# Recurrence output of a fused audio-tower layer: one clamped exponential, no GpSimd products, divisor and sigmoid inverted together

## The chip, the cores and the metric

The kernel runs on one core of a Trainium2 chip, as one program from inputs in memory to output in memory. The metric is the device time of one execution in microseconds (us). The engines are TensorE (PE: matmuls and transposes), VectorE (DVE), ScalarE (ACT: activation functions), GpSimd (POOL) and SyncE (SP, which issues most DMAs here). Each engine runs its own list of instructions in order and meets the others only through semaphores.

## The reference

The input x is 32 sequences of 750 steps with 256 channels, float32.

```
h = wavelet low pass with stride 2, twice, along time          # 32 x 750 x 256 -> 32 x 192 x 256
n = layernorm(h);  k = n @ Wk.T;  r = n @ Wr.T;  v = r
w = -exp(time_decay);  u = time_first                          # per channel
for each step t:                                               # (a, b, pp) start at 0, 0, -1e38
    q  = max(pp, u + k_t);  e1 = exp(pp - q);  e2 = exp(u + k_t - q)
    y_t = (e1 * a + e2 * v_t) / (e1 * b + e2)
    q2 = max(pp + w, k_t);  f1 = exp(pp + w - q2);  f2 = exp(k_t - q2)
    a, b, pp = f1 * a + f2 * v_t, f1 * b + f2, q2
h = h + (sigmoid(r) * y) @ Wo.T
n2 = layernorm(h);  the 2 best of 8 experts by n2 @ router_w + router_b, gates by softmax
h = h + sum over the two of gate * (relu(n2 @ W1 + b1) @ W2 + b2)
```

## The kernel before, in words

The program has two stages. `tokens_to_experts` does everything up to the routing, `experts` does the expert matmuls, the gather of tokens by lists and the accumulation into the output. The change touches only the first.

The first stage takes the 32 sequences two at a time, as 16 pairs. The five steps of a pair are spread over five rounds: `rounds` calls `body(p0, p1, p2, p3, p4)` for rounds 0 to 19 on every engine, with pair p0 in step 0 (wavelet filter and layernorm statistics), p1 in step 1 (transposes and the projections k and r), p2 in step 2 (the recurrence), p3 in step 3 (output projection, second layernorm) and p4 in step 4 (routing, token lists). A step whose pair doesn't exist in a round is left out: p2 exists in rounds 2 to 17 and p4 in rounds 4 to 19.

With channels on partitions, a pair is 128 x 4 rows (two halves of the channels, two sequences) of 192 steps, so most recurrence tiles have 768 elements in a partition, or 772 where one column is put in front. DVE works the recurrence as scans along time: `pp` (add and max) at L605, `sbb` and `sa` (multiply and add) at L643 and L646. Around them stand, in the kernel before:

- `dl` = k + u - pp (L613, two instructions, since u differs by half), `dn_s` (L621, two), and on ACT `up_s`, `e2s`, `e1s` (L367 to L371) for the state, and `e2y`, `e1y` (L380, L383: a relu and an exponential each) for the output.
- POOL forms the products `t2` = e2y * v (L332) and `t3` = e1y * sbb (L338); DVE forms `t1` = e1y * sa (L666), `num` = t1 + t2 (L681), `den` = t3 + e2y (L690) and `dsg` = den * (1 + exp(-r)) (L693, with `er` from L385 and L683).
- ACT forms `inv` = exp(-ln(dsg)) (L428, L431), and in the next round DVE forms `oT` = num * inv (L628, two instructions).

POOL also runs a chain of four tiny operations for each layernorm (`rstd`, L319 to L325), from the statistics that DVE's `bn_aggr` (L587) gives to the scale and bias that ACT uses, and at the end of its round it issues six indirect DMAs (L346) that write the token lists of p4. They wait for the 24th of the 25 routing steps. The routing steps are small DVE instructions on 3 to 24 elements (among them `is_second`, L759); `route_to(k)` issues those up to number k, which scatters them between the large ones of the round.

PE's order in a round is: the first part of the wavelet (`conv_first`, L468), the transposes for p1, `project(p3)` (L483, which waits for oT), the rest of the wavelet (`conv_rest`, L474), k and r for p1 with `ranks` between them, the transposes for p3, the last of r, and the router logits (L530). ACT copies the finished wavelet to `h` (L389); DVE takes `bn_stats` of it (L672) for p0.

Of the kernel before, what the change touches and what calls it, by code (L numbers as in the profile page):

```python
# [22 lines left out]
ALU = mybir.AluOpType  # L23
# [8 lines left out]
P = 128  # L32
# [34 lines left out]
EMAX = 2.0 ** 54  # L67

# [63 lines left out]
def tokens_to_experts(nc, x, taps, taps_down, wkT, wrT, woT, decay, first, rw, rb, out, rows, lists, tables):  # L132
# [12 lines left out]
    with ctx:  # L145
# [4 lines left out]
        w, uw, nuw = sb("w", [P, HC]), sb("uw", [P, HC]), sb("nuw", [P, HC])  # L150
# [11 lines left out]
        c_eps, c_pow, c_neg = sb("c_eps", [P, 3]), sb("c_pow", [P, 3]), sb("c_neg", [P, 3])  # L162
        zrow, nobody = sb("zrow", [P, R * C]), sb("nobody", [P, LIST // P], U32)
# [49 lines left out]
        setup_act, pads = sem("setup_act"), sem("pads")  # L213
        x_loaded = [sem("x_loaded0"), sem("x_loaded1")]
# [9 lines left out]
        diffs, clamped, exps, state, t2_done, t3_done = sem("diffs"), sem("clamped"), sem("exps"), sem("state"), sem("t2_done"), sem("t3_done")  # L224
# [5 lines left out]
        N_LN1, N_LN2, N_DIFF, N_STATE, N_ROUTE, N_RSTD = 6, 7, 5, 8, 25, 4  # L230
# [64 lines left out]
        def _(pool):  # L295
# [948 lines left out]
```

## Time and profile before

| | |
|---|---|
| median of 3 runs | 1180.82 us |
| lowest, highest | 1174.84, 1181.34 us |
| profiled execution: span from first to last instruction | 1179.9 us |
| first stage | up to about 412 us of the span |
| busy share of the span: PE, DVE, ACT, POOL | 85%, 79%, 56%, 62% |
| mean granted TensorE clock | 0.934 of full |

The profiled execution is one execution; its span is 0.9 us under the median of the runs. The shares are means over both stages, which have different limits, so the stage has to be read by itself: by busy time in a window, and by the order of instructions in time.

### The profile page before, as it was taken

To read this page: it belongs to the slowest core of one execution; us is meant where nothing else is said; L and a number is where in the kernel's file an instruction comes from. 1 tells how busy PE (TensorE), PEld (TensorE's weight loads), DVE (VectorE), ACT (ScalarE), POOL (GpSimd) and SP (SyncE) were. 2 spreads that over 40 slices of the span, in tenths; PEclk is the share of its full clock that TensorE was granted. 3 is DMA by queue.
4 is the path that set the end of the run, shared out by engine and by line. 5 is a ranking of instruction groups with operands and counts; after the bars stand their busy time and mean duration, and the time that the engine had idled before them with its cause. 6 is when DMAs were issued, how large, how long until landed. Compare 5 with 4: busy or idle time off the path is not lost.

```text
span 1179.9 us, 21997 instructions
## 1 busy us (share of the span) xinstructions
PE 1008.8 (85%) x6244; PEld 917.8 (78%) x6244; DVE 931.9 (79%) x2350; ACT 656.6 (56%) x1253; POOL 735.6 (62%) x634
## 2 busy tenths in 40 slices
PE   6878878887874329999999999999999999999994
PEld 5656646666643229999999999999999999999994
DVE  2899999999998437878778877878878788787872
ACT  2767757666755125556555555555555555555651
POOL 1458778778778434565665657566565655656563
PEclk9898998888976559999999999999999999999997
DMA  7334235235111145565655647565574655646572
GB/s 240 99 97 132 82 100 141 81 94 131 43 41 41 41 175 171 133 189 146 171 177 131 188 129 190 152 163 182 126 191 135 182 168 144 187 127 188 147 170 29
DMA packets 76131, 160.78 MB, mean 136 GB/s; under 512 B 12781, under 2 KB 65518, under 8 KB 70986
## 3 DMA queue, kind: packets, MB, share of 16 engines
q0 software_dynamic: 34592, 120.55, 37.3%
q1 hardware_dynamic: 41514, 39.95, 11.6%
q8 instruction: 10, 0.16, 0.1%
q14 instruction: 15, 0.12, 0.0%
HBM read 131.81 MB, written 28.65 MB: 136 GB/s over the span
## 4 chain that ended last, share of the span: by engine, by line
issue 15%; POOL 15%; DVE 12%; PE 10%; DMA 8%; DVEq 1%; ACT 1%; POOLq 1%; ACTq 0%
POOL out_rows L995 8%; DMA out_rows<-yout,dest 7%; PE acc L1083 5%; PE hp L1072 5%; DVE wlo L1120 3%; POOL b2s L958 3%; POOL tid L948 3%; DVE ysum L1197 3%; DVE hhi L1172 2%; DVE xlo L1124 1%; DVE hlo L1174 1%; DMA raw<-in_ew,idx 1%; POOL raw L945 1%; DVE gA L1140 1%; PE xt L1063 0%
## 5 line engine op out<-in xcount | busy, mean ns | idle before, releaser
L1041 ACT ACTIVATE hid<-hp,b 128x384 f32<-128x384 f32 x312 | 180.4, 578 | 318.7 <-PE hp L1072 318.1
L1083 PE MATMUL acc<-whi,hhi 128*128 128x256 f32 x936 | 266.2, 284 | 29.4 <-DVE hlo L1174 29.4
L1083 PE MATMUL acc<-wlo,hhi 128*128 128x256 f32 x936 | 261.5, 279 | 0.0
L1083 PE MATMUL acc<-whi,hlo 128*128 128x256 f32 x936 | 261.4, 279 | 0.0
L1072 PE MATMUL hp<-xhi,whi 128*128 128x384 f32 x624 | 215.4, 345 | 2.2 <-DVE xlo L1124 2.2
L995 POOL DMA_INDIRECT out_rows<-yout,dest x117 | 185.8, 1588 | 47.7 <-issue 35.1
L1120 DVE TENSOR_TENSOR wlo<-raw,whi 128x512 fp32r<-128x512 f32 x312 | 213.0, 684 | 0.8 <-ACT whi L1016 0.8
L1072 PE MATMUL hp<-xlo,whi 128*128 128x384 f32 x624 | 211.0, 338 | 0.0
L1072 PE MATMUL hp<-xhi,wlo 128*128 128x384 f32 x624 | 211.0, 338 | 0.0
L1016 ACT ACTIVATE whi<-raw 128x512 fp32r<-128x512 f32 x312 | 194.3, 624 | 28.7 <-DMA raw<-in_ew,idx 28.7
L1083 PEld LDWEIGHTS acc<-whi,hhi 128*128 128x128 f32 x936 | 175.4, 187 | 42.6 <-issue 27.7
L1172 DVE CAST hhi<-hid 128x384 fp32r<-128x384 f32 x312 | 117.1, 375 | 83.3 <-ACT hid L1041 75.4
L1174 DVE TENSOR_TENSOR hlo<-hid,hhi 128x384 fp32r<-128x384 f32 x312 | 174.1, 558 | 10.8
L1083 PEld LDWEIGHTS acc<-wlo,hhi 128*128 128x128 f32 x936 | 175.8, 188 | 0.0
L1083 PEld LDWEIGHTS acc<-whi,hlo 128*128 128x128 f32 x936 | 175.6, 188 | 0.0
L945 POOL DMA_INDIRECT raw<-in_ew,idx x40 | 46.9, 1172 | 176.0 <-issue 165.3
L954 POOL DMA_INDIRECT xg<-token_rows,tid x120 | 125.2, 1043 | 46.7 <-issue 44.0
L346 POOL DMA_INDIRECT expert_lists<-tid,slots x96 | 131.6, 1371 | 30.9 <-issue 26.2
L1072 PEld LDWEIGHTS hp<-xhi,whi 128*128 128x128 f32 x624 | 117.8, 189 | 3.7 <-DVE xlo L1124 2.6
L1072 PEld LDWEIGHTS hp<-xhi,wlo 128*128 128x128 f32 x624 | 118.0, 189 | 0.0
L1072 PEld LDWEIGHTS hp<-xlo,whi 128*128 128x128 f32 x624 | 117.6, 188 | 0.0
L468 PE MATMUL conv_ps<-xin,filt 128*128 128x256 f32 x256 | 67.4, 423 | 3.0 <-DVE wseq L576 1.6
(174 smaller groups left out, 1715.9 us busy)
## 6 DMA issues: line engine op xcount, KB each, us to landing
xin<-in_x SPq DMA_DIRECT2D x32, 512.0 KB
xin<-in_x SPq DMA_DIRECT2D x32, 256.0 KB
token_rows<-xs SPq DMA_DIRECT2D x16, 259.0 KB
out_rows<-h SPq DMA_DIRECT2D x16, 256.0 KB, 3.3
token_rows<-xs SPq DMA_DIRECT2D x32, 64.8 KB
out_rows<-h SPq DMA_DIRECT2D x32, 64.0 KB, 4.1
xg<-token_rows,tid POOLq DMA_INDIRECT x120
out_rows<-yout,dest POOLq DMA_INDIRECT x117
```

The costliest lines, as they stand in the source:

```text
L346: pool.indirect_dma_start(lists, bass.IndirectOffsetOnAxis(slots[:, p4.s, c:c + 1], 0), tid[:, p4.s, c % 3:c % 3 + 1], None).then_inc(list ...
L468: pe.matmul(conv_ps[:, b * C:(b + 1) * C], filt[:, s, :], xin[:, q.s, b, s, :], start=s == 0, stop=s == K_FIRST - 1)
L945: pool.indirect_dma_start(raw[:, j.s, :], None, ew, bass.IndirectOffsetOnAxis(idx[:, j.s, 0:1], 0)).then_inc(w_in[j.s], 16)
L954: pool.indirect_dma_start(xg[:, j.s, r, :], None, rows, bass.IndirectOffsetOnAxis(tid[:, j.s, r:r + 1], 0)).then_inc(x_in[j.s], 16)
L995: pool.indirect_dma_start(out[:, :], bass.IndirectOffsetOnAxis(dest[:, j.s, r:r + 1], 0), yout[:, j.s, r, :], None, compute_op=ALU.add).th ...
L1016: act.activation(whi[:, j.s, k * PIECE:(k + 1) * PIECE], raw[:, j.s, k * PIECE:(k + 1) * PIECE], ACT.Copy).then_inc(whi_done, 1)
L1041: act.activation(hid[:, c % 2, :], hp[c % 2][:, 0:TS], ACT.Relu, bias=b1[:, j.s, c:c + 1]).then_inc(hid_done, 1)
L1072: last = pe.matmul(hp[c % 2][:, 0:TS], w_[:, j.s, at:at + P], x_[:, j.s, k, :], start=n == 0, stop=n == 3 * HC - 1)
L1083: last = pe.matmul(acc[r][:, 0:C], h_[:, c % 4, r * P:(r + 1) * P], w_[:, j.s, at:at + C], start=c == 0 and n == 0, stop=c == FC - 1 and n ...
L1120: dve.tensor_tensor(wlo[:, j.s, a], raw[:, j.s, a], whi[:, j.s, a].bitcast(F32), ALU.subtract).then_inc(wlo_done, 1)
L1172: dve.tensor_copy(hhi[:, c % 4, :], hid[:, c % 2, :]).then_inc(hhi_done, 1)
L1174: dve.tensor_tensor(hlo[:, c % 4, :], hid[:, c % 2, :], hhi[:, c % 4, :].bitcast(F32), ALU.subtract).then_inc(hlo_done, 1)
```

## The change

- `dl` loses u and is one subtraction of 768 elements: k - pp. The two distances for the state both come from ACT, as relu(dl - w's size) and relu(w's size - dl) (four relus into `dist`), and one exponential of 1536 elements makes both `e1s` and `e2s`. `dn_s` and `up_s` go.
- The output uses the unclamped ratio: `ey` = exp(dl + u), two activations by half. DVE clamps it at CAP = 2^55 inside `t2` = min(ey, CAP) * v and div[0] = min(ey, CAP) + sbb, and adds `num` = t2 + sa. POOL's products t2 and t3 and DVE's t1, den and dsg go.
- Divisor (div[0]) and 1 + exp(-r) (div[1]) are inverted together: one Ln and one Exp of 1536 elements on ACT. DVE then multiplies num by inv[0] and, in the two `oT` instructions, by inv[1].
- For the first step of each sequence, the state before it is given by two seeds that POOL writes in each round, ahead of its rstd chains: the first column of `kpad` is k_1 - 30, the first column of `e2sv` is v_1. DVE's scan `pp` waits for the first seed, its scan `sa` for the second (semaphore `seeded`).
- On DVE the `bn_stats` of p0 move from behind t1 to behind oT, ahead of e2sv and the two state scans. The numbers in the `route_to` calls are set anew; the last steps of the routing stand at the end of the round.

```diff
# POOL
             def body(p0, p1, p2, p3, p4):
                 if p2:
-                    pool.wait_ge(exps, p2.at(4, 3))
+                    pool.wait_ge(kr_taken, p2.at(4, 2))
+                    pool.tensor_tensor(kpad[:, p2.s, :, 0:1], kpad[:, p2.s, :, 1:2], c_before[:, :, :], ALU.add).then_inc(seeded, 1)
                     pool.wait_ge(kr_taken, p2.at(4, 4))
                     pool.wait_ge(state, p2.at(N_STATE))
-                    pool.tensor_tensor(t2[:, :, :], e2y[:, :, :], v[:, p2.s], ALU.mult).then_inc(t2_done, 1)
+                    pool.tensor_tensor(e2sv[:, :, 0:1], v[:, p2.s, :, 0:1], c_one[:, :, :], ALU.mult).then_inc(seeded, 1)
                 if p3:
                     rstd(p3, ln2, N_LN2, mv2, ve2, rs2, mr2, nb2, rstd2)
-                if p2:
-                    pool.wait_ge(exps, p2.at(4, 4))
-                    pool.wait_ge(state, p2.at(N_STATE, 2))
-                    pool.tensor_tensor(t3[:, :, :], e1y[:, :, :], sb_[:, :, 0:T], ALU.mult).then_inc(t3_done, 1)
                 if p0:
...
# ACT
                 if p2:
                     act.wait_ge(state, p2.at(N_STATE))
-                    act.wait_ge(t3_done, p2.at(1))
-                    for k in range(HC):
-                        act.wait_ge(diffs, p2.at(N_DIFF, 2 + k))
-                        a = slice(2 * k, 2 * k + 2)
-                        act.activation(up_s[:, a, :], dl[:, a, :], ACT.Relu, bias=nuw[:, k:k + 1]).then_inc(clamped, 1)
-                    act.wait_ge(diffs, p2.at(N_DIFF, 5))
-                    act.activation(e2s[:, :, 1:TP], dn_s[:, :, :], ACT.Exp).then_inc(exps, 1)
-                    act.wait_ge(clamped, p2.at(4, 2))
-                    act.activation(e1s[:, :, 1:TP], up_s[:, :, :], ACT.Exp, scale=-1.0).then_inc(exps, 1)
+                    act.wait_ge(diffs, p2.at(N_DIFF, 2))
+                    for n, (sign, bias) in enumerate(((1.0, nw), (-1.0, w))):
+                        for k in range(HC):
+                            a = slice(2 * k, 2 * k + 2)
+                            act.activation(dist[:, n, a, :], dl[:, a, :], ACT.Relu, bias=bias[:, k:k + 1], scale=sign).then_inc(clamped, 1)
+                    act.wait_ge(clamped, p2.at(4, 4))
+                    act.activation(es[:, :, :, 1:TP], dist[:, :, :, :], ACT.Exp, scale=-1.0).then_inc(exps, 1)
...
                 if p2:
-                    for sign, dst in ((-1.0, e2y), (1.0, e1y)):
-                        act.activation(dst[:, :, :], dl[:, :, :], ACT.Relu, scale=sign).then_inc(clamped, 1)
-                    for k, dst in enumerate((e2y, e1y)):
-                        act.wait_ge(clamped, p2.at(4, k + 3))
-                        act.activation(dst[:, :, :], dst[:, :, :], ACT.Exp, scale=-1.0).then_inc(exps, 1)
+                    for k in range(HC):
+                        a = slice(2 * k, 2 * k + 2)
+                        act.activation(ey[:, a, :], dl[:, a, :], ACT.Exp, bias=u[:, k:k + 1]).then_inc(exps, 1)
...
-                    act.activation(lnd[:, :], dsg[:, :], ACT.Ln).then_inc(inv_ready, 1)
+                    act.activation(lnd[:, :, :], div[:, :, :], ACT.Ln).then_inc(inv_ready, 1)
...
-                    act.activation(inv[:, :], lnd[:, :], ACT.Exp, scale=-1.0).then_inc(inv_ready, 1)
+                    act.activation(inv[:, :, :], lnd[:, :, :], ACT.Exp, scale=-1.0).then_inc(inv_ready, 1)
```

DVE's round after the change, cut to its large instructions and the waits that matter (the part of p3 between `route_to(14)` and `route_to(18)` is as before: h1, bn_stats, bn_aggr, with routing steps 15 to 18 between them):

```python
                if p2:
                    dve.wait_ge(kr_taken, p2.at(4, 2))
                    dve.wait_ge(seeded, p2.at(2, 1))
...
                    dve.tensor_tensor_scan(flat(pp), flat(wseq), kpad[:, p2.s].rearrange("p a t -> p (a t)"), NEG,
                                           ALU.add, ALU.max).then_inc(diffs, 1)
                route_to(1)
                if p2:
...
                    dve.tensor_tensor(dl[:, :, :], kpad[:, p2.s, :, 1:TP], pp[:, :, 0:T], ALU.subtract).then_inc(diffs, 1)
                route_to(2)
                if p3:
                    dve.wait_ge(inv_ready, p3.at(2, 2))
...
                    dve.tensor_tensor(num[:, :], num[:, :], inv[:, 0, :], ALU.mult).then_inc(o_ready, 1)
                    route_to(4)
...
                            i.rearrange("p (k b t) -> p k b t", k=HC, b=2)[:, :, :, a] for i in (num[:, :], inv[:, 1, :])),
                            ALU.mult).then_inc(o_ready, 1)
                        route_to(5 + n)
                route_to(7)
                if p0:
                    dve.wait_ge(h_taken, p0.at(1, 1))
...
                    for t in range(3):
                        dve.bn_stats(st1[:, t, :], tile_of_h(p0, t)).then_inc(ln1, 1)
                        route_to(8 + t)
                    dve.wait_ge(rstd1, p0.at(N_RSTD))
                    aggregate(p0, st1, mv1, N_LN1, 3, ln1)
                route_to(11)
                if p2:
...
                    dve.tensor_tensor(e2sv[:, :, 1:TP], e2s[:, :, 1:TP], v[:, p2.s], ALU.mult).then_inc(state, 1)
                    route_to(12)
                    dve.tensor_tensor_scan(flat(sb_), e1s.rearrange("p a t -> p (a t)"), e2s.rearrange("p a t -> p (a t)"), 0.0,
                                           ALU.mult, ALU.add).then_inc(state, 1)
                    route_to(13)
                    dve.wait_ge(state, p2.at(N_STATE, 1))
                    dve.wait_ge(seeded, p2.at(2, 2))
                    dve.tensor_tensor_scan(flat(sa), e1s.rearrange("p a t -> p (a t)"), flat(e2sv), 0.0, ALU.mult, ALU.add).then_inc(state, 1)
                route_to(14)
                if p3:
...
                route_to(18)
                if p2:
                    dve.wait_ge(exps, p2.at(N_EXP, 3))
                    dve.scalar_tensor_tensor(out=t2[:, :, :], in0=ey[:, :, :], scalar=CAP, in1=v[:, p2.s],
                                             op0=ALU.min, op1=ALU.mult).then_inc(state, 1)
                    route_to(20)
...
                    dve.scalar_tensor_tensor(out=div[:, 0, :].rearrange("p (a t) -> p a t", t=T), in0=ey[:, :, :], scalar=CAP,
                                             in1=sb_[:, :, 0:T], op0=ALU.min, op1=ALU.add).then_inc(state, 1)
                    route_to(22)
...
                    dve.tensor_tensor(num[:, :].rearrange("p (a t) -> p a t", t=T), t2[:, :, :], sa[:, :, 0:T], ALU.add).then_inc(state, 1)
                    route_to(23)
                    dve.wait_ge(er_ready, p2.at(1, 1))
                    dve.tensor_scalar(div[:, 1, :], er[:, :], EMAX, 1.0, ALU.min, ALU.add).then_inc(state, 1)
                route_to(N_ROUTE)
```

## Rows read from the trace of the kernel before

**Rows 1.** Windows: stretch, then busy us (and instructions) of PE, PEld, DVE, ACT, POOL; granted clock; DMA

```profile
67.52:358.56 291.04, 235.73 (x1036) 176.62 (x1035) 275.11 (x697) 195.94 (x350) 222.59 (x201) 0.89 0.32 90
```

**Rows 2.** DVE in order of time: the scan that opens a round (start, duration, instruction)

```profile
29.91 1.77 DVE L605 TENSOR_TENSOR_SCAN pp<-wseq,kpad 128x772 f32<-128x772 f32 x1 [0.51 <-ACT kpad L401]
...
47.50 1.76 DVE L605 TENSOR_TENSOR_SCAN pp<-wseq,kpad 128x772 f32<-128x772 f32 x1
...
67.52 1.76 DVE L605 TENSOR_TENSOR_SCAN pp<-wseq,kpad 128x772 f32<-128x772 f32 x1
...
337.26 1.76 DVE L605 TENSOR_TENSOR_SCAN pp<-wseq,kpad 128x772 f32<-128x772 f32 x1
...
358.56 1.76 DVE L605 TENSOR_TENSOR_SCAN pp<-wseq,kpad 128x772 f32<-128x772 f32 x1
```

**Rows 3.** POOL in order of time, round 1 and a full round

```profile
31.74 0.19 POOL L325 TENSOR_TENSOR nb<-mr,c_neg 128x3 f32<-128x3 f32 x1
...
202.46 2.31 POOL L346 DMA_INDIRECT expert_lists<-tid,slots  x1 [0.17 <-issue]
...
211.76 1.44 POOL L346 DMA_INDIRECT expert_lists<-tid,slots  x1 [0.30 <-issue]
213.23 1.81 POOL L332 TENSOR_TENSOR t<-e2y,v 128x768 f32<-128x768 f32 x1
...
221.04 0.90 POOL L319 TENSOR_TENSOR ve<-mv,c_eps 128x3 f32<-128x3 f32 x1
...
223.68 0.92 POOL L325 TENSOR_TENSOR nb<-mr,c_neg 128x3 f32<-128x3 f32 x1
```

**Rows 4.** DVE's groups by form, 67.52 to 358.56 us (count, busy us, mean ns)

```profile
L681 DVE TENSOR_TENSOR num<-t 128x768 f32<-128x768 f32 x13 | 29.5, 2266 | 0.0
...
L759 DVE TENSOR_TENSOR oh<-cand,i 128x24 f32<-128x24 f32 x13 | 16.7, 1288 | 0.0
L613 DVE SCALAR_TENSOR_TENSOR dl<-kpad,u,pp 128x384 f32<-128x384 f32 x26 | 16.0, 615 | 0.1
...
L693 DVE TENSOR_TENSOR dsg<-den,er 128x768 f32<-128x768 f32 x14 | 13.4, 958 | 0.5
...
L621 DVE TENSOR_SCALAR dn_s<-dl,uw 128x384 f32<-128x384 f32 x26 | 11.6, 447 | 0.0
L628 DVE TENSOR_TENSOR oT<-num,inv 128x512 f32<-128x512 f32 x13 | 8.8, 679 | 1.5 <-ACT inv L431 1.5
...
L628 DVE TENSOR_TENSOR oT<-num,inv 128x256 f32<-128x256 f32 x13 | 5.4, 414 | 0.0
```

**Rows 5.** DVE in order of time, the same round as in group 3

```profile
213.29 1.80 DVE L759 TENSOR_TENSOR oh<-cand,i 128x24 f32<-128x24 f32 x1
```

**Rows 6.** ACT's groups by form, 67.52 to 358.56 us

```profile
L367 ACT ACTIVATE up_s<-dl,nuw 128x384 f32<-128x384 f32 x26 | 14.4, 600 | 0.0
```

**Rows 7.** ACT in order of time, the same round

```profile
210.58 0.84 ACT L383 ACTIVATE e2y<-e2y 128x768 f32<-128x768 f32 x1
```

**Rows 8.** POOL in order of time, round 18, where DVE has little work

```profile
391.91 0.19 POOL L319 TENSOR_TENSOR ve<-mv,c_eps 128x3 f32<-128x3 f32 x1 [7.16 <-DVE mv L587]
...
393.41 0.19 POOL L325 TENSOR_TENSOR nb<-mr,c_neg 128x3 f32<-128x3 f32 x1
394.14 1.03 POOL L346 DMA_INDIRECT expert_lists<-tid,slots  x1 [0.54 <-issue]
...
400.52 0.96 POOL L346 DMA_INDIRECT expert_lists<-tid,slots  x1 [0.30 <-issue]
```

**Rows 9.** PE and ACT in order of time, a full round: output projection to the copy of h

```profile
233.82 2.76 PE L483 MATMUL wo_ps<-wo,oT 128*128 128x256 f32 x12
236.41 1.89 PE L474 MATMUL conv_ps<-xin,filt_rest 128*128 128x256 f32 x8
...
238.51 0.81 ACT L389 ACTIVATE h<-conv_ps 128x768 f32 x1 [0.29 <-PE conv_ps L474]
```

**Rows 10.** PE in order of time, the output projection of round 17

```profile
363.82 5.44 PE L483 MATMUL wo_ps<-wo,oT 128*128 128x256 f32 x12 [3.66 <-DVE oT L628]
```

More of the change, by code:

```diff
@@ L176, in tokens_to_experts @@
         dl = sb("dl", [P, SEQ, T])
-        up_s, dn_s = sb("up_s", [P, SEQ, T]), sb("dn_s", [P, SEQ, T])
-        e1s, e2s, e2sv = sb("e1s", [P, SEQ, TP]), sb("e2s", [P, SEQ, TP]), sb("e2sv", [P, SEQ, TP])
-        e1y, e2y = sb("e1y", [P, SEQ, T]), sb("e2y", [P, SEQ, T])
+        dist = sb("dist", [P, 2, SEQ, T])
+        es, e2sv = sb("es", [P, 2, SEQ, TP]), sb("e2sv", [P, SEQ, TP])
+        e1s, e2s = es[:, 0], es[:, 1]
+        ey = sb("ey", [P, SEQ, T])
         sa, sb_ = sb("sa", [P, SEQ, TP]), sb("sbb", [P, SEQ, TP])
-        t1, t2, t3 = (sb(n, [P, SEQ, T]) for n in ("t1", "t2", "t3"))
-        num, den, dsg = (sb(n, [P, SEQ * T]) for n in ("num", "den", "dsg"))
-        lnd, inv = sb("lnd", [P, SEQ * T]), sb("inv", [P, SEQ * T])
+        t2, num = sb("t2", [P, SEQ, T]), sb("num", [P, SEQ * T])
+        div = sb("div", [P, 2, SEQ * T])
+        lnd, inv = sb("lnd", [P, 2, SEQ * T]), sb("inv", [P, 2, SEQ * T])
         oT = sb("oT", [P, HC, 3 * P])
@@ L309, in _ @@
             pool.memset(c_neg[:, :], -1.0).then_inc(pads, 1)
-            pool.memset(kpad[:, :, :, 0:1], NEG).then_inc(pads, 1)
-            for pad in (e1s, e2s, e2sv):
-                pool.memset(pad[:, :, 0:1], 0.0).then_inc(pads, 1)
+            pool.memset(es[:, 0, :, 0:1], 0.0).then_inc(pads, 1)
+            pool.memset(es[:, 1, :, 0:1], 1.0).then_inc(pads, 1)
+            pool.memset(c_one[:, :, :], 1.0).then_inc(pads, 1)
+            pool.memset(c_before[:, :, :], BEFORE).then_inc(pads, 1)
             pool.wait_ge(pads, 9)
@@ L355, in _ @@
             act.wait_ge(params, 32)
-            act.activation(w[:, :], dec[:, :], ACT.Exp).then_inc(setup_act, 1)
-            act.wait_ge(consts, 13)
+            act.activation(nw[:, :], dec[:, :], ACT.Exp).then_inc(setup_act, 1)
+            act.wait_ge(consts, 11)
             def body(p0, p1, p2, p3, p4):
@@ L609, in body @@
                     dve.wait_ge(clamped, p2.at(4))
-                    for k in range(HC):
-                        dve.wait_ge(diffs, p2.at(N_DIFF, 1))
-                        a = slice(2 * k, 2 * k + 2)
-                        dve.scalar_tensor_tensor(out=dl[:, a, :], in0=kpad[:, p2.s, a, 1:TP], scalar=u[:, k:k + 1], in1=pp[:, a, 0:T],
-                                                 op0=ALU.add, op1=ALU.subtract).then_inc(diffs, 1)
-                        route_to(2 + k)
-                if p2:
-                    dve.wait_ge(exps, p2.at(4))
-                    for k in range(HC):
-                        dve.wait_ge(diffs, p2.at(N_DIFF, 2 + k))
-                        a = slice(2 * k, 2 * k + 2)
-                        dve.tensor_scalar(dn_s[:, a, :], dl[:, a, :], uw[:, k:k + 1], 0.0, ALU.subtract, ALU.min).then_inc(diffs, 1)
-                        route_to(4 + k)
+                    dve.wait_ge(exps, p2.at(N_EXP))
+                    dve.wait_ge(diffs, p2.at(N_DIFF, 1))
+                    dve.tensor_tensor(dl[:, :, :], kpad[:, p2.s, :, 1:TP], pp[:, :, 0:T], ALU.subtract).then_inc(diffs, 1)
+                route_to(2)
                 if p3:
@@ L679, in body @@
+                    dve.scalar_tensor_tensor(out=div[:, 0, :].rearrange("p (a t) -> p a t", t=T), in0=ey[:, :, :], scalar=CAP,
+                                             in1=sb_[:, :, 0:T], op0=ALU.min, op1=ALU.add).then_inc(state, 1)
+                    route_to(22)
                     dve.wait_ge(state, p2.at(N_STATE, 4))
[L680 to L681 removed]
+                    dve.wait_ge(o_ready, p2.at(N_OUT))
```

84 lines of the change are left out of this document (31 added, 53 removed).

## The prediction

> **What bounds the kernel now.** I read the share of busy time by stretch first, then the order of time on the engines. The change touches only the first stage, in which twenty rounds of the loop carry sixteen pairs of sequences through five steps; the expert stage behind it stays as it is. Between the third and the last state scan pass 291.04 us for 13 rounds, and VectorE (DVE) is busy for 275.11 of them [rows 1]. So a round lasts 291.04 / 13 = 22.39 us, of which DVE works 21.16, ScalarE (ACT) 15.1, GpSimd (POOL) 17.1 and TensorE (PE) 18.1. The starts of the scan that opens each round say the same: 17.6 and 20.0 us for the first two rounds, which carry fewer pairs, then (337.26 - 67.52) / 12 = 22.48 for rounds with all five steps, and 21.30 for the last, which loads no new pair [rows 2]. DVE is the bound, and nothing waits long.
>
> POOL is the engine to look at in order of time. It takes each round's six indirect DMAs (the writing of the token lists) one after the other: from 202.46 to 213.17 us they hold it for 10.7 us. Its next instruction, the product t2 of the following round, starts at 213.23, 0.06 us after the last DMA [rows 3]. POOL runs in order and an indirect DMA occupies it until it has been issued. Today that costs nothing, because DVE asks for t2 only near the end of its round.
>
> **What the change removes and adds on DVE.** Prices are means over the 13 rounds [rows 4]. For dl, two instructions of 0.615 us become one without a scalar; at the price of the 768-element form without a stall, 0.96, that is 0.27 less. The two dn_s (0.447 each) go: 0.89. The product num times inv is added: 0.96. t1 and den are of the form of dsg and go with it: 3 x 0.96 = 2.87. Two instructions come that clamp ey and multiply or add. Their form is shown only with 384 elements, at 0.615; the two oT products (512 and 256 elements, 0.679 and 0.414) give 1.04 ns for an element, so 768 elements need about 0.615 + 384 x 0.00104 = 1.01, together 2.03. The addition num stays, and falls from 2.27 to 0.96, and the routing step is_second falls from 1.29 to about 0.17. Both are held up today: is_second, on 24 elements, takes 1.80 us at 213.29, and ends 0.05 us after the POOL product that began at 213.23 [rows 3, 5]. So with the products gone 1.31 + 1.12 = 2.43 us come back. In all: -0.27 - 0.89 + 0.96 - 2.87 + 2.03 - 2.43 = -3.5, and a round's work on DVE falls from 21.2 to 17.7 us.
>
> The Trainium skill (SBUF - State Buffer, section "Who interferes with whom") has this as a rule: a DVE instruction with two SBUF inputs and a GpSimd instruction that reads SBUF lock each other out for the whole instruction. The trace agrees, at 1.80 us for a step that needs 0.17. By the rule the products' removal is a pure gain, and it says nothing of the queue behind the DMAs, on which the sum below turns.
>
> **What it adds on ACT.** Two more relus of 384 elements (0.60 each), one exponential of 1536 elements for two of 768 (0.84 each), two exponentials of 384 for two relus and two exponentials of 768, and a Ln and an Exp of 1536 elements where 768 stood: +1.2, 0, about -2.1, +1.4 [rows 6, 7]. ACT stays near 15.6 us in a round and bounds nothing by its sum.
>
> **The first new wait: the seed.** POOL now writes the first column of kpad (kpad[1] - 30), and DVE's first instruction of the round, the scan, waits for it. That seed is the first instruction of POOL's round, and so stands behind the six DMAs of the round before. These wait for the 24th routing step, and in the new order of DVE that step is among the very last of its round. Nothing is left to DVE to hide the DMAs under. It stands for their whole length. With DVE idle six of them take 394.14 to 401.48 = 7.34 us, shorter than the 10.7 beside a working DVE [rows 3, 8]. I take 7.3 and add 0.2 ahead of the first and 0.3 for the seed and its two signals (a POOL operation on a few elements takes 0.19 when DVE is idle [rows 8]).
>
> **The second: POOL is late at the DMAs.** After the statistics of step three (aggr of p3), POOL has both rstd chains to run, since the p0 chain stands behind the p3 chain. DVE then has left t2, div, num, er and seven routing steps, about 4.0 us. A chain takes 3.56 us beside a working DVE (221.04 to 224.60) and 1.69 beside an idle one (391.91 to 393.60) [rows 3, 8]. The first at 3.5 and the second, half of it beside DVE, at 2.5 end 2.0 us after DVE. Ends: 0 (both unhindered, 3.4) and 3.1 (both hindered, 7.1).
>
> **The third: bn_stats moved up.** The three bn_stats of p0 now stand behind oT and ahead of e2sv and the two scans. They need h, which ACT copies after conv_rest, and PE puts conv_rest behind project(p3), which needs oT. From the end of oT: project and conv_rest run from 233.82 to 238.30, the copy of h from 238.51 to 239.32 [rows 9]. That is 5.5 us in which DVE has one routing step to do, where today a state product, two scans and more lie in between. ACT's own line, from dl over four relus (2.0), the long exponential (1.5), xnT, ey and er (2.5), comes to h after 6.0, against 2.3 + 4.7 = 7.0 by PE, so PE's counts. I take 5.5. The upper end: project has also taken 5.44 [rows 10], and conv_rest slowed in the same ratio 3.7, which makes 10.0. In the new round PE runs logits, conv_first and transposes just ahead of project, as before 233.82, where it was fast; so I take the fast one. The lower end is 4.5, if some of it overlaps. On SP, the store of xs waits for routing step 21 and the loads of x stand behind it; both come later in the round by the new order, but the x loaded is that of the next use of its buffer, two rounds on: nothing.
>
> **The sum.** A full round: 17.7 (work) + 5.5 (h) + 2.0 (POOL late) + 0.2 + 7.3 (DMAs) + 0.3 (seed) = 33.0, against 22.48: +10.5. There are 12 of them, from the scan of round 4 to that of round 16, since every one follows a round with routing: +126 us. The interval from round 16 to 17 has no p0: without bn_stats (1.5), without the wait for h, with one rstd chain, but 1.3 us until the exponential is ready: 17.7 - 1.5 + 1.3 + 7.8 = 25.3 against 21.30, +4. The first two intervals have no DMAs. The scan at 29.91 now stands behind the rstd chain of the round before, which ends at 31.93 beside it and would end some 0.7 earlier without it (+1.6 with the seed) [rows 2, 3]; the wait for h makes that round another 1.3 longer; the next has the wait for h and POOL's lateness, without routing steps, and PE was slow there: +6. Together +9, between +5 and +12. In the tail, DVE's round after the last scan is 3.5 shorter, and longer Ln and Exp (1.4) and the added product (1.0) come twice on its path: about 0 net. Total 126 + 4 + 9 + 0 = 139. The profiled execution has a span of 1179.9, one us under the median of 1180.82, so the forecast is **1320 us**.
>
> **The rivals.**
> (a) PE runs slowly at project and conv_rest in most rounds: +4.5 a round, 12 x 4.5 = 54, so 1370. For it: PE idles more in a longer round, and 5.44 us is seen after 3.66 us of idling [rows 10]. Against it: 2.76 at 233.82, straight after conv_first.
> (b) The seed costs nothing, because the DMAs free POOL at once; the waits for h remain. A round is 17.7 + 5.5 = 23.2 and some gaps, about 23.6: 13 x 1.1 + 9 = 23, so 1204. Against it: the product at 213.23 begins only as the last DMA ends though ACT had written its input e2y by 211.42 [rows 3, 7]. The Trainium skill (DMA: Bandwidth & Descriptors, section "SWDGE vs HWDGE vs iDMA") says that a GpSimd core computes such a DMA's descriptors in software, which speaks against (b) as the rows do.
> (c) Faster: the work counts and no wait does. DVE's round falls by 3.5 to about 18.9 with its gaps, still above PE's 18.1: -3.5 x 13 = -46, so 1135. It is one mechanism, the DVE's work as the only bound, and it decides if the seed leaves POOL before the DMAs: they would need 7.3 us or more of DVE work behind routing step 24, and there are none.
>
> **How the numbers follow.** Chances: the forecast 0.76, (a) 0.12, (b) 0.07, (c) 0.05. The bounds of the forecast: POOL late 0 instead of 2.0 and h after 4.5 give 30.0 a round, 12 x -3.0 = -36, and the start -4, which would be 1280; both at their lowest at once is unlikely, and half of it is taken: 1298. Upwards (a) at its full price is 1370, and POOL's 3.1 adds 13 more; the range goes to 1372. Faster by over 1%: 0.05. Within 1%, which is about what a measurement of this kernel can tell from no change: 0.02, from (b) at its cheapest. Slower: 0.93.
>
> **What would show it.** Right: DVE idle ahead of the scan of a full round for 9 to 10 us, released by POOL's operation on kpad; idle again for about 5 us ahead of the bn_stats of p0, released by ACT's h; the six DMAs at 0.96 each; scans 33 us apart; no routing step above 0.3 us; the expert stage as long as before. The DVE's new clamped instructions should be 1.0 each. Wrong: the seed released early, with scans 24 us apart (b), or project at 5.4 in most rounds and scans 37 apart (a). The prediction would also fail if POOL could take the seed before a DMA that still waits for its routing step; the order in which it issues is fixed by the program, so I give that nothing beyond (b) and (c).

## The result, and the profile after

The changed kernel takes 1336.18 us (median of 4 runs, 1335.21 to 1338.7), the kernel before 1180.92 beside it: a ratio of 1.132 with an interval of 1.129 to 1.135. The profiled execution has a span of 1333.3 us at a mean granted clock of 0.874, against 1179.9 at 0.934. The forecast was 1320, range 1298 to 1372.

The expert stage begins with the same instruction in both, a copy of the list indices on DVE, at 420.67 us before and at 578.23 after. By that the first stage is 157.6 us longer, and the expert stage 4.2 us shorter (755.1 against 759.2). Its code is the same in every run here, and in the profiled executions of all of them it takes 755.0 to 759.2 us, so these 4.2 us aren't put down to the change. The twelve rounds from the scan of round 4 to that of round 16, before and after, by windows (stretch, length, then busy us of PE, PEld, DVE, ACT, POOL; granted clock; DMA); [rows 1] go one round further, to the scan of round 17:

```profile
67.52:337.26 269.74, 220.12 (x978) 165.44 (x978) 255.65 (x649) 181.53 (x324) 205.17 (x188) 0.90 0.34 94
```

```profile
77.92:489.67 411.75, 291.55 (x1012) 211.00 (x1011) 214.14 (x613) 193.59 (x321) 129.83 (x193) 0.73 0.22 63
```

411.75 / 12 = 34.31 us for a round, against 22.48 [rows 2]. DVE works 214.14 / 12 = 17.85 of it, 3.5 less than before (255.65 / 12 = 21.30). It now idles for nearly half of each round, and TensorE's granted clock falls from 0.90 to 0.73. DVE in order of time, one round (it answers to [rows 2, 5]):

```profile
275.67 0.17 DVE L800 TENSOR_SCALAR tok<-tok 128x3 f32<-128x3 f32 x1
285.53 1.77 DVE L601 TENSOR_TENSOR_SCAN pp<-wseq,kpad 128x772 f32<-128x772 f32 x1 [9.70 <-issue]
...
296.77 0.43 DVE L628 BATCH_NORM_STATS2 st<-h 128x6 f32 x1 [5.80 <-ACT h L387]
...
319.28 1.77 DVE L601 TENSOR_TENSOR_SCAN pp<-wseq,kpad 128x772 f32<-128x772 f32 x1 [9.70 <-issue]
```

Two brackets hold the loss: 9.70 us ahead of the scan and 5.80 ahead of the bn_stats of p0. The first is put down to "issue", that is, to nothing the profile names. POOL in order of time shows what it was (it answers to [rows 3, 8]):

```profile
277.09 0.20 POOL L331 TENSOR_TENSOR nb<-mr,c_neg 128x3 f32<-128x3 f32 x1
277.89 1.03 POOL L349 DMA_INDIRECT expert_lists<-tid,slots  x1 [0.61 <-issue]
...
284.30 0.96 POOL L349 DMA_INDIRECT expert_lists<-tid,slots  x1 [0.31 <-issue]
285.28 0.21 POOL L336 TENSOR_TENSOR kpad<-kpad,c_before 128x4 f32<-128x4 f32 x1
```

DVE's last instruction of the round ends at 275.84. POOL's second rstd chain ends 1.45 us later, the first DMA issues at 277.89, the last is issued at 285.26, and the seed runs at 285.28. The scan starts inside the 0.25 us that follow. DVE's groups by form over the twelve rounds (count | busy us, mean ns | idle before them and its releasers; to be set beside [rows 4]):

```profile
L601 DVE TENSOR_TENSOR_SCAN pp<-wseq,kpad 128x772 f32<-128x772 f32 x13 | 23.0, 1767 | 118.9 <-issue 109.2 <-POOL kpad L336 9.7
L628 DVE BATCH_NORM_STATS2 st<-h 128x6 f32 x30 | 12.6, 422 | 61.6 <-ACT h L387 61.6
...
L669 DVE SCALAR_TENSOR_TENSOR div<-ey,sbb 128x768 f32<-128x768 f32 x12 | 11.4, 952 | 0.0
...
L674 DVE TENSOR_TENSOR num<-t,sa 128x768 f32<-128x768 f32 x12 | 11.3, 945 | 0.0
L664 DVE SCALAR_TENSOR_TENSOR t<-ey,v 128x768 f32<-128x768 f32 x12 | 11.1, 926 | 0.0
L628 DVE BATCH_NORM_STATS2 st<-h 128x6 f32<-128x256 f32 x6 | 2.5, 422 | 10.9 <-ACT h L387 10.9
L744 DVE TENSOR_TENSOR oh<-cand,i 128x24 f32<-128x24 f32 x12 | 2.1, 177 | 0.0
```

The 118.9 counts thirteen scans; 2.20 of it stand ahead of the first, which opens the stretch. So 116.7 / 12 = 9.7 us a round stand ahead of the scan, and (61.6 + 10.9) / 12 = 6.0 ahead of bn_stats. The addition num fell from 2.27 to 0.945 and is_second from 1.29 to 0.177: the gains are there, and they are small beside the waits.

### The profile page after: what moved, and what is told of

Same layout as the page of the kernel before. It is cut to its first block, busy times and chain, and to the rows that moved or that the text cites. A ratio compares the mean times of both kernels' runs of the same rounds, so it can differ in the third digit from the quotient of the medians.

```text
span 1333.3 us, 21822 instructions
## 1 busy us (share of the span) xinstructions
PE 1070.0 (80%) x6244; PEld 956.8 (72%) x6244; DVE 877.8 (66%) x2300; ACT 664.5 (50%) x1237; POOL 635.2 (48%) x634
## 4 chain that ended last, share of the span: by engine, by line
issue 14%; POOL 13%; DVE 11%; PE 10%; DMA 6%; DVEq 1%; ACT 1%; POOLq 1%; ACTq 0%
POOL out_rows L980 7%; DMA out_rows<-yout,dest 6%; PE acc L1068 5%; PE hp L1057 4%; DVE wlo L1105 3%; POOL b2s L943 3%; POOL tid L933 3%; DVE ysum L1182 2%; DVE hhi L1157 2%; DVE xlo L1109 1%; DVE hlo L1159 1%; DMA raw<-in_ew,idx 1%; POOL raw L930 1%; DVE gA L1125 1%; PE xt L1048 0%
## 5 line engine op out<-in xcount | busy, mean ns | idle before, releaser
L325 POOL TENSOR_TENSOR ve<-mv,c_eps 128x3 f32<-128x3 f32 x32 | 15.8, 493 | 335.8 <-DVE mv L582 327.1
L1157 DVE CAST hhi<-hid 128x384 fp32r<-128x384 f32 x312 | 114.4, 367 | 81.7 <-ACT hid L1026 74.1
L601 DVE TENSOR_TENSOR_SCAN pp<-wseq,kpad 128x772 f32<-128x772 f32 x16 | 28.3, 1766 | 129.3 <-issue 117.5
```

Source lines behind the costliest of these rows:

```text
L1157: dve.tensor_copy(hhi[:, c % 4, :], hid[:, c % 2, :]).then_inc(hhi_done, 1)
```

## The experiments

The forecast's waits were confirmed as such. The open question was whether each is worth what it shows. Theory A: they add up, so that removing one gives its idle time back. Theory B: they lie beside chains over PE (statistics of p3, rstd, xs, transposes, logits, conv_first, project) and over ACT (x2T, xn, copies of v, Ln, Exp) that end nearly as late, so that only both together give the time back. Ratios are to the kernel before, rounds are means over the twelve from the scan of round 4 to that of round 16.

**e1_seed_early.** After, with the seed for the next pair written ahead of the DMAs.

```diff
@@ POOL, body @@
-                if p2:
-                    pool.wait_ge(kr_taken, p2.at(4, 2))
-                    pool.tensor_tensor(kpad[:, p2.s, :, 0:1], kpad[:, p2.s, :, 1:2], c_before[:, :, :], ALU.add).then_inc(seeded, 1)
...
                     rstd(p0, ln1, N_LN1, mv1, ve1, rs1, mr1, nb1, rstd1)
+                if p1:
+                    pool.wait_ge(kr_taken, p1.at(4, 2))
+                    pool.tensor_tensor(kpad[:, p1.s, :, 0:1], kpad[:, p1.s, :, 1:2], c_before[:, :, :], ALU.add).then_inc(seeded, 1)
                 if p4:
```

> The changed kernel (1336 us), but POOL writes the kpad seed of the next pair ahead of the six DMAs of its round, not behind them. Theory A (the two waits add up, as in my sum): the 9.7 us of idling ahead of the scan go, 12 rounds fall from 34 to about 24.5, and the time is near 1220 us. Theory B (the waits lie beside one another: the chain from the p3 statistics over rstd, xs, transposes, x2T, xn, logits and conv_first on PE, and over Ln and Exp on ACT, ends almost when the seed does): DVE waits at the first routing step and at num times inv in place of the seed, a round is 31 to 33.5 us, and the time is 1295 to 1325 us. I expect B.

1304.02 us, ratio 1.106 (1.102 to 1.110); a round is 31.44. DVE in order of time:

```profile
231.31 1.77 DVE L602 TENSOR_TENSOR_SCAN pp<-wseq,kpad 128x772 f32<-128x772 f32 x1 [1.65 <-POOL kpad L345]
237.07 0.18 DVE L698 TENSOR_TENSOR lg<-cnt_ps,rbs 128x24 f32<-128x24 f32 x1 [3.99 <-PE cnt_ps L529]
239.02 0.96 DVE L614 TENSOR_TENSOR num<-num,inv 128x768 f32<-128x768 f32 x1 [0.77 <-ACT inv L430]
247.45 0.43 DVE L629 BATCH_NORM_STATS2 st<-h 128x6 f32 x1 [5.77 <-ACT h L388]
```

Of 9.7 us ahead of the scan 8.0 are gone, and 2.9 came back. In this round DVE now waits 3.99 for the logits and 0.77 for inv, and the wait for h is as long as ever. That is B. The 2.9 is a mean of two kinds of round. Where conv_first runs in 3.70 us, as in this one, a round is mostly 30.5, and 3.3 came back against the 33.75 of most rounds before the edit. In three rounds (33.6 to 33.8) conv_first takes 6.4 to 6.7 and nothing came back. DVE in such a round:

```profile
329.55 0.18 DVE L698 TENSOR_TENSOR lg<-cnt_ps,rbs 128x24 f32<-128x24 f32 x1 [4.89 <-PE cnt_ps L529]
342.07 0.43 DVE L629 BATCH_NORM_STATS2 st<-h 128x6 f32 x1 [8.71 <-ACT h L388]
```

So the slow TensorE is part of why the early seed alone gives so little. In the changed kernel most rounds have the slow conv_first too, but there it runs while DVE waits for the seed.

**e2_stats_back.** After, with the bn_stats of p0 behind the statistics of p3 and the product t2, where they stood before.

```diff
@@ DVE, body @@
-                if p0:
-                    dve.wait_ge(h_taken, p0.at(1, 1))
...
                         dve.bn_stats(st2[:, t, :], h1[:, p3.s, t, :]).then_inc(ln2, 1)
...
+                if p0:
+                    dve.wait_ge(h_taken, p0.at(1, 1))
+                    dve.wait_ge(ln1, p0.at(N_LN1))
+                    dve.sem_inc(stats_seen, 1)
+                    for t in range(3):
+                        dve.bn_stats(st1[:, t, :], tile_of_h(p0, t)).then_inc(ln1, 1)
+                        route_to(19 + t)
+                    dve.wait_ge(rstd1, p0.at(N_RSTD))
+                    aggregate(p0, st1, mv1, N_LN1, 3, ln1)
```

> The changed kernel, but the bn_stats of p0 stand where they stood before the change (behind the p3 statistics), with the routing steps dealt out as before the change. The seed stays behind the DMAs. My sum: the wait for h (5.8 us, 7.4 in some rounds) goes and nothing takes its place but the wait for es of about 1 us: a round falls from 34.3 to 28 us, the time is 1250 to 1270 us. If the seed's wait grew by what the other gives (the rival), the time would stay within 1% of 1336.

1257.73 us, ratio 1.066 (1.063 to 1.069); a round is 28.37. DVE's groups by form:

```profile
L601 DVE TENSOR_TENSOR_SCAN pp<-wseq,kpad 128x772 f32<-128x772 f32 x13 | 23.0, 1766 | 106.1 <-POOL kpad L336 86.9 <-issue 19.2
L628 DVE TENSOR_TENSOR e2sv<-es,v 128x768 f32<-128x768 f32 x12 | 11.5, 959 | 12.9 <-ACT es L372 12.9
```

The wait for h is gone and nearly all of it came back: 5.9 a round. Of the 106.1 ahead of the scans 1.5 belong to the first, so the seed still costs 104.6 / 12 = 8.7 us.

**e3_both_back.** Both edits.

> Both edits together: seed ahead of the DMAs, bn_stats back. Work alone (17.7 to 18.2 us and gaps on DVE) would give rounds of 19 to 20 us and about 1145 us. By theory B the chain from the p3 statistics to inv (13 us) and on over oT, project and h1 back to these statistics (9 to 10 us) is left: rounds of 22 to 23.5 us, 1175 to 1205 us, so about the time of the kernel before the change, with DVE idle at num times inv or at h1.

1187.16 us (9 runs), ratio 1.005 (1.003 to 1.007); a round is 22.49. Alone the two edits gave 2.9 and 5.9 us a round, together 11.8, of 15.7 that the brackets show. So nearly all of the loss comes from the two waits: with both edits the kernel is within 1% of the one before. Windows and DVE's groups by form, twelve rounds:

```profile
71.53:341.35 269.82, 218.85 (x988) 164.43 (x986) 216.95 (x612) 187.00 (x315) 150.85 (x186) 0.92 0.34 95
```

```profile
L602 DVE TENSOR_TENSOR_SCAN pp<-wseq,kpad 128x772 f32<-128x772 f32 x12 | 21.2, 1767 | 8.8 <-POOL kpad L345 6.6 <-issue 1.5 <-ACT v L400 0.7
L629 DVE TENSOR_TENSOR e2sv<-es,v 128x768 f32<-128x768 f32 x12 | 11.7, 979 | 10.7 <-ACT es L373 10.7
L614 DVE TENSOR_TENSOR num<-num,inv 128x768 f32<-128x768 f32 x12 | 11.5, 956 | 12.9 <-ACT inv L430 12.9
L697 DVE TENSOR_TENSOR lg<-cnt_ps,rbs 128x24 f32<-128x24 f32 x12 | 2.2, 183 | 16.7 <-PE cnt_ps L529 16.7
```

DVE's work is 18.1 us a round, 3.2 less than before, and the round is as long as before: the saved work has turned into four waits of 4.0 us together (49.1 in these rows, less 1.5 ahead of the first scan, over 12). What holds the round was the next question. The trace of e3 has a loop over four engines with hardly any slack in it:

```profile
227.21 0.49 ACT L415 ACTIVATE x2T<-tp_ps 128x384 f32<-128x384 f32 x1 [1.16 <-PE tp_ps L458]
...
237.15 0.99 DVE L629 TENSOR_TENSOR e2sv<-es,v 128x768 f32<-128x768 f32 x1 [0.86 <-ACT es L373]
...
244.42 1.04 POOL L325 TENSOR_TENSOR ve<-mv,c_eps 128x3 f32<-128x3 f32 x1 [6.22 <-DVE mv L583]
...
247.09 1.58 ACT L409 ACTIVATE xs<-h,nb,rs 128x256 f32<-128x256 f32 x3 [1.66 <-POOL nb L331]
...
249.54 0.49 ACT L415 ACTIVATE x2T<-tp_ps 128x384 f32<-128x384 f32 x1 [0.86 <-PE tp_ps L458]
```

From x2T ACT works until es ends at 236.94 (but for 0.1 us), 9.7 us; DVE then takes 7.2 from e2sv to the statistics of p3, POOL 2.6 for rstd, ACT 1.6 for xs, PE under 1 for the transposes. That makes 22.33 us from x2T to x2T, the length of a round.

**e4_products_cut.** The kernel before, with POOL's two products on one column (the rest of t2 and t3 is a constant 0.5), to price what they cost DVE.

```diff
@@ POOL, body @@
-                    pool.tensor_tensor(t2[:, :, :], e2y[:, :, :], v[:, p2.s], ALU.mult).then_inc(t2_done, 1)
+                    pool.tensor_tensor(t2[:, :, 0:1], e2y[:, :, 0:1], v[:, p2.s, :, 0:1], ALU.mult).then_inc(t2_done, 1)
...
-                    pool.tensor_tensor(t3[:, :, :], e1y[:, :, :], sb_[:, :, 0:T], ALU.mult).then_inc(t3_done, 1)
+                    pool.tensor_tensor(t3[:, :, 0:1], e1y[:, :, 0:1], sb_[:, :, 0:1], ALU.mult).then_inc(t3_done, 1)
```

> The kernel before the change (1181 us) with POOL's two products cut to the first column of each row (t2 and t3 are filled with 0.5 once at the start, so the output is not the reference's). It leaves out 191 of 192 columns of both products. If DVE's work alone bounds the old rounds, the 2.4 us for which the products hold num and is_second come back in each of 13 rounds: 1150 us, with num at 0.95 and is_second at 0.17 us. If the chain over inv is as long as DVE's round (theory B for the old kernel), little of it arrives: 1165 to 1180 us, and DVE idles ahead of oT.

1155.8 us, ratio 0.979 (0.976 to 0.982). DVE's groups by form:

```profile
L683 DVE TENSOR_TENSOR num<-t 128x768 f32<-128x768 f32 x12 | 11.5, 958 | 0.0
L761 DVE TENSOR_TENSOR oh<-cand,i 128x24 f32<-128x24 f32 x12 | 2.2, 180 | 0.0
```

Both stalls are gone, and the round falls from 22.48 to 20.68: 1.8 of the 2.4 us reach it. In the same rounds DVE waits 15.4 / 12 = 1.3 us for the logits, so PE's chain is close behind. The edit also frees POOL, so it doesn't price DVE's work quite by itself.

**e5_inv_before_xn.** e3, with Ln and Exp ahead of xn and of the last copy of v on ACT, dl ahead of the routing steps on DVE, and the seed ahead of the rstd chain of p0 on POOL.

```diff
@@ ACT, body, loop over k @@
                         act.activation(x2T[:, k, :], x2_ps[k], ACT.Copy).then_inc(t2T_taken, 1)
+                    if p2 and k == 1:
...
+                        act.activation(lnd[:, :, :], div[:, :, :], ACT.Ln).then_inc(inv_ready, 1)
...
+                        act.activation(inv[:, :, :], lnd[:, :, :], ACT.Exp, scale=-1.0).then_inc(inv_ready, 1)
                     if p0 and k == 1:
```

> The kernel with the seed ahead of the DMAs and bn_stats back (1187 us, rounds of 22.5 us), and three more edits: the first routing steps stand behind num times inv instead of ahead of dl, the seed stands ahead of the p0 rstd chain, and on ACT Ln and Exp stand ahead of the scaling to xn and of the last copy of v. If the chain over inv bounds the round, it gets about 2 us shorter: rounds of 20.5 to 21 us, 1160 to 1172 us. If PE's chain (transposes, last of r, logits, wavelet, project) is as long, DVE idles at h1 instead and the time stays above 1175 us.

1184.71 us (10 runs), ratio 1.0015 (0.9998 to 1.003); a round is 22.35. A miss of the gain, and neither of the two expected causes alone: DVE in order of time waits for es.

```profile
230.32 0.96 DVE L612 TENSOR_TENSOR num<-num,inv 128x768 f32<-128x768 f32 x1 [1.72 <-issue]
235.89 0.96 DVE L627 TENSOR_TENSOR e2sv<-es,v 128x768 f32<-128x768 f32 x1 [2.32 <-ACT es L373]
```

ACT works from x2T at 225.98 to the end of es at 235.67, with one gap of 0.20 us. This block is as long as in e3 (9.7 us); only the order in it had changed, and the wait went from its one product to its other. The loop from x2T to x2T is as long as before, and so is the round.

**e6_project_first** and **e7_inv_after_xs.** e5 with PE's order project, transposes of p1, conv_first, conv_rest; and e6 with Ln and Exp straight behind xs, ahead of x2T.

```diff
@@ PE, body (e6) @@
-                if p0:
-                    conv_first(p0)
+                if p3:
+                    project(p3)
                 if p1:
...
-                if p3:
-                    project(p3)
                 if p0:
+                    conv_first(p0)
                     conv_rest(p0)
```

> The same with PE's order changed: project and the transposes of p1 ahead of the first part of the wavelet. If PE's chain is what is left, rounds fall to 19.5 to 20.5 us and the time to 1145 to 1160 us; if the wait for oT now holds the wavelet and h comes too late for bn_stats, it is no better than the one before, 1160 to 1185 us.

> As the one before (project first), but Ln and Exp on ACT stand right behind the scaling to xs, ahead of the copies x2T. inv is ready another 1 us earlier, the logits 3 us later. If inv bounds, 1140 to 1155 us; if the logits and what follows them on PE bound, 1 us a round is lost and it is 10 us or more slower than the one before.

1209.78 us, ratio 1.021 (1.019 to 1.024), and 1231.68, ratio 1.042 (1.039 to 1.045): misses, both slower. PE in order of time, the first line of e6, the second of e7:

```profile
226.47 5.48 PE L482 MATMUL wo_ps<-wo,oT 128*128 128x256 f32 x12 [3.90 <-issue]
```

```profile
233.30 2.72 PE L528 MATMUL cnt_ps<-rws,x2T 128*128 128x8 f32 x12 [3.68 <-ACT x2T L421]
```

With nothing in front of it to fill the time, project takes 5.48 us after 3.90 us of idling, against 2.76 in [rows 9]: twice the time, the lower of TensorE's two clock levels (1.2 and 2.4 GHz). Ln and Exp ahead of x2T make the logits, and all of PE's round behind them, wait.

**e8_three_dmas.** After, with three indirect DMAs in a round; it leaves out the lists of the second choices.

```diff
-                    for c in range(6):
+                    for c in range(3):
```

> The changed kernel (1336 us) with three indirect DMAs in each round instead of six. It leaves out the token lists of the second choice, so half of the list entries stay at the row of nobody; the expert stage handles as many tiles. If the seed waits for the issue of the DMAs, the idle time ahead of the scan falls by 3 x 1.26 = 3.8 us, from 9.7 to 5.9. By theory B the PE chain is next after 1 to 3.5 us of it, so rounds are 30.5 to 33.6 us as with the early seed, and the time is about 1300 us, not 1336 - 13 x 3.8 = 1287. If the wait for the seed had another cause than the issue, it would stay at 1336.

1300.1 us, ratio 1.098 (1.096 to 1.101); a round is 31.79. DVE in order of time:

```profile
237.19 1.77 DVE L601 TENSOR_TENSOR_SCAN pp<-wseq,kpad 128x772 f32<-128x772 f32 x1 [5.89 <-POOL kpad L336]
249.04 0.43 DVE L628 BATCH_NORM_STATS2 st<-h 128x6 f32 x1 [5.78 <-ACT h L387]
```

Three DMAs less take 3 x 1.27 = 3.8 us off the wait for the seed (9.70 to 5.89), which shows that the scan waits for the DMAs' issue; 2.5 of them reach the round.

**e9_xn_after_es.** e5, with the copy of v ahead of Ln, and with xn (ACT) and the transposes of p1 (PE) moved out of the block, behind es and behind conv_rest; the copies xnT follow behind h.

> From the kernel with inv ahead of xn (1185 us, rounds of 22.48 us, DVE idle 2.3 us ahead of e2sv because ACT does inv, xn, the last copy of v, the four relus and es in one stretch): xn of a pair goes behind es of the next round, the last copy of v ahead of Ln, the copies xnT behind h, and on PE the transposes of p1 behind the rest of the wavelet. If ACT's stretch bounds the round, es is ready 1.6 us sooner and rounds fall to 20.7 us: 1184.7 - 13 x 1.6 = about 1163 us. If something else is as long (PE at the slower clock, or the later xnT and with it kpad), 1175 to 1185 us.

1184.1 us (12 runs), ratio 0.998 (0.995 to 1.002); a round is 21.99: a miss. The wait for es fell to 0.4 us, and others came: inv, which the copy of v now precedes (2.4 us a round, 1.5 in e5), and the seed of e2sv, which still stands behind the DMAs. DVE in order of time:

```profile
232.30 1.77 DVE L634 TENSOR_TENSOR_SCAN sa<-es,e2sv 128x772 f32<-128x772 f32 x1 [0.96 <-issue]
```

**e10_both_seeds_early.** e9, with the seed of e2sv for the next pair ahead of the DMAs too.

```diff
@@ POOL, body @@
+                if p1:
+                    pool.wait_ge(kr_taken, p1.at(4, 4))
+                    if p2:
+                        pool.wait_ge(state, p2.at(N_STATE, 3))
+                    pool.tensor_tensor(e2sv[:, :, 0:1], v[:, p1.s, :, 0:1], c_one[:, :, :], ALU.mult).then_inc(seeded, 1)
                 if p4:
```

> The kernel with xn behind es (1184 us, rounds of 21 to 23 us), and the second seed too (e2sv, behind the DMAs so far) written for the next pair ahead of the DMAs. In half of its rounds the scan sa waits 0.96 us for that seed. If it is on the path, 13 rounds lose 0.5 to 1 us: 1170 to 1178 us. If the DMAs, which now also stand behind the last copy of v, come in the way of the next rstd chain, nothing is gained.

1172.84 us (6 runs), ratio 0.991 (0.987 to 0.994), inside the 1170 to 1178 expected; a round is 21.80. Three of the twelve rounds are long, 24.06, 24.46 and 24.46 us, and in these conv_first takes 5.5 to 6.6 us; the other nine are 20.96 in the mean.

**e11_clamp_on_dve.** e10, with one of the two clamps on DVE, and each exponential started by its own clamp.

```diff
@@ ACT, body @@
-                    for n, (sign, bias) in enumerate(((1.0, nw), (-1.0, w))):
...
-                    act.activation(es[:, :, :, 1:TP], dist[:, :, :, :], ACT.Exp, scale=-1.0).then_inc(exps, 1)
+                    for k in range(HC):
+                        a = slice(2 * k, 2 * k + 2)
+                        act.activation(dist[:, 0, a, :], dl[:, a, :], ACT.Relu, bias=nw[:, k:k + 1]).then_inc(clamped, 1)
...
+                    act.activation(e2s[:, :, 1:TP], dist[:, 1], ACT.Exp).then_inc(exps, 1)
...
+                    act.activation(e1s[:, :, 1:TP], dist[:, 0], ACT.Exp, scale=-1.0).then_inc(exps, 1)
@@ DVE, behind dl @@
+                        dve.tensor_scalar(dist[:, 1, a, :], dl[:, a, :], w[:, k:k + 1], 0.0, ALU.subtract, ALU.min).then_inc(diffs, 1)
```

> As the one before, but the distance for e2s comes from DVE again (two small instructions of 0.45 us, as dn_s before the change), and ACT makes two relus and two exponentials of 768 elements instead of four relus and one of 1536. ACT's stretch from x2T to es gets 1.0 us shorter, DVE's work 0.9 longer. If ACT's stretch bounds the round (DVE idles 1.5 to 3.5 us in it), a round is 0.8 us shorter again: about 10 us under the one before, 1160 to 1168 us. If DVE's work bounds, it is 5 to 10 us slower than the one before.

1159.71 us (6 runs), ratio 0.979 (0.976 to 0.982): faster than both kernels. Windows, the twelve rounds:

```profile
65.98:316.37 250.39, 202.61 (x993) 149.95 (x992) 225.91 (x637) 177.05 (x304) 167.85 (x188) 0.99 0.39 104
```

DVE works more than in e3 (18.8 us a round against 18.1) and the round is 1.6 shorter (20.87). That speaks against DVE's work as the bound, and fits the loop through ACT. But the granted clock is 0.99 against 0.93 in e10, conv_first never takes over 3.70, and the 0.93 us that a round gained over e10 are about what e10's three long rounds cost. How much is ACT's shorter stretch by itself and how much TensorE's clock, these runs don't separate.

## Why the prediction was right

**What bounds.** DVE's work as the bound of before is borne out by e4: without its two stalls of 2.4 us the round is 1.8 shorter.

**The removed and added work.** 17.7 us was forecast, 17.85 measured. The clamped instructions take 0.93 and 0.95 (forecast 1.01), num 0.945 (0.96), is_second 0.177 (0.17). Ln and Exp of 1536 elements take 1.48 each.

**The seed and POOL's lateness.** 2.0 + 0.2 + 7.3 + 0.3 = 9.8 was forecast, 9.7 measured. e8 shows the mechanism by its size, e1 by its place. That the sum is so close is in part luck. POOL ends 1.45 after DVE (forecast 2.0), since the second chain ran almost unhindered; and 0.61 stands ahead of the first DMA (forecast 0.2, though [rows 8] have 0.54 there). The two errors cancel. The DMAs take 7.37, and 0.27 follow. The rows of before put the last DMA's end at 213.20, not 213.17, which changes nothing.

**bn_stats moved up.** 5.5 was forecast, 6.0 measured, and e2 gives 5.9 back. Half of the excess comes from the two rounds with a slow project, in which the wait is 7.4.

**The size.** The sum of a full round was 33.0, and 34.31 was measured. The terms of the two waits and the work explain 17.85 + 9.7 + 6.0 = 33.6, of which 0.6 are mis-sized terms (the wait for h 0.5, the work 0.15, the seed -0.1). The remaining 0.7 us was no term at all: small gaps between dependent instructions, and two waits in the first interval, which lasts 37.73. DVE in that interval:

```profile
82.95 0.18 DVE L697 TENSOR_TENSOR lg<-cnt_ps,rbs 128x24 f32<-128x24 f32 x1 [3.26 <-PE cnt_ps L528]
85.12 0.96 DVE L613 TENSOR_TENSOR num<-num,inv 128x768 f32<-128x768 f32 x1 [1.01 <-ACT inv L429]
```

The round before it has no DMAs, so its seed is ready early and the scan waits only 2.20. DVE then waits for the logits and for inv, 4.3 us, which in later rounds are ready by the time the seed is. That is 0.36 of the 0.7, and it is theory B's chains, seen in the changed kernel itself.

The twelve rounds came to +142 (forecast +126), the start to +10.4 (+9), the interval from round 16 to 17 to 25.81 (25.3), so +4.5 (+4), and the rest of the first stage to +0.6 (0). These make 157.6, where 139 was forecast. The expert stage was 4.2 shorter in these two executions, which leaves 153.4. That brought the total nearer to the forecast, and no term of the sum had foreseen it.

**The range.** Its upper end doesn't follow from its own terms: 1320 + 54 is 1374 and not 1370, and the 13 us for POOL's lateness were named and then left out. With them it would be 1387. Half of the way down to 1280 is 1300 and not 1298. The measured time lies inside either way.

**Rival (a), PE slow.** PE in order of time, a round with a slow and a round with a fast project:

```profile
246.97 3.70 PE L466 MATMUL conv_ps<-xin,filt 128*128 128x256 f32 x16
255.55 4.48 PE L481 MATMUL wo_ps<-wo,oT 128*128 128x256 f32 x12 [4.22 <-DVE oT L618]
...
283.86 6.53 PE L466 MATMUL conv_ps<-xin,filt 128*128 128x256 f32 x16
290.88 2.76 PE L481 MATMUL wo_ps<-wo,oT 128*128 128x256 f32 x12
293.48 1.89 PE L472 MATMUL conv_ps<-xin,filt_rest 128*128 128x256 f32 x8
```

Most rounds are of the second kind, as taken: the slow part falls on conv_first (6.53), and project runs at 2.76 behind it. Project takes 4.5 us in two of the twelve rounds (255.55 and 392.10), and those are the two intervals of 35.25 us, where most last 33.75; that is the small part of (a) that came. The first interval, 37.73, has a project of 2.86 and is long for the other reason, told above.

**Where the reasoning was weak, though the total hid it.** Rival (b), the seed free and only the waits for h left, was priced at 1204. With the seed moved ahead of the DMAs the kernel takes 1304: the price left out what is late next, the logits and inv, and a slow conv_first where it comes. Rival (c), the work counts and no wait does, was priced at 1135. With both waits gone e3 takes 1187: 3.2 us less work on DVE was worth nothing, because the loop through ACT's stretch from x2T to es then bounds the round. The change itself lengthened that stretch. In the kernel before ACT works 6.6 us from x2T to the end of e2s (200.02 to 207.75, less 1.15 of waiting); in e3 it works 9.6, since Ln and Exp, the relus and the exponential of 1536 elements all stand in it. The prediction said that ACT bounds nothing by its sum, which holds for the changed kernel, and didn't ask what ACT's order holds up. Both prices subtracted a wait or a work from DVE's line alone and did not ask which chain on PE or ACT ends next. Idle brackets of one engine added up well to a slowdown and badly to a gain.

## What to carry to other kernels

Before a small operation is given to an in-order engine, read what it is queued behind: here 0.2 us of work on POOL cost up to 9.7 us a round, since six indirect DMAs stood in front of it, and written one step earlier, with bn_stats back in place, it left a wait of 0.7. To price a slowdown, adding the new waits on the bounding engine came within an eighth (139 of 157.6 us); to price their removal, follow the chains on the other engines too, since two waits worth 2.9 and 5.9 alone were worth 11.8 together. When work taken off the bounding engine brings nothing, find the engine with an unbroken stretch ahead of the next wait, follow the loop back to that stretch, and try to move work off it (e11; how much of its gain is due to that isn't shown).

## What was not expected of the hardware

**An indirect DMA that starts just behind a scan's start ends only after the scan.** POOL in order of time, e3, where DVE's scan (two SBUF inputs) runs from 227.73 to 229.50:

```profile
228.25 2.09 POOL L350 DMA_INDIRECT expert_lists<-tid,slots  x1 [0.56 <-issue]
230.64 0.96 POOL L350 DMA_INDIRECT expert_lists<-tid,slots  x1 [0.31 <-ACT v L400]
```

It ends at 230.34, 0.84 after the scan. So it is in every one of e3's thirteen rounds with the first DMA beside that scan (0.83 to 1.01 after it). In the kernel before, the DMA at 202.46 [rows 3] ends at 204.77, 0.86 after the scan that ends at 203.91. With DVE idle it takes 0.96. Over the twelve rounds the mean is 1.28 us in e3, 1.43 before and 0.98 after. It was otherwise where the DMA came first: five DMAs of the kernel before that started 0.13 us ahead of a state scan took 0.95 or 0.96, as if DVE were idle. The timing fits a POOL that is held for as long as the scan runs; no run tried it by itself.

**TensorE's low clock falls on the work behind a pause, and the order of PE moves it.** The granted clock over the twelve rounds is 0.73 in the changed kernel, 0.92 in e3, 0.99 in e11. Within the rounds shown the slow project stands behind a pause: 5.48 in e6 after 3.90 us without work, 4.48 after 4.22, and 2.76 when conv_first ran in front of it. What a slow group costs depends on what waits beside it: a conv_first of 6.5 costs the changed kernel nothing under the wait for the seed (rounds of 33.75), and costs e1, with that wait gone, 3.2 us (33.7 against 30.5). An order of PE that looks better on paper (e6) lost 25 us to e5 for this reason among others.
